# Edge network of a four-layer graph kernel: the head-wise scaling of the message norm in one VectorE operation per tile and head, GpSimd left with the bias

## The reference, cut to what matters

```python
for h in range(4):
    K_v, V_v = x @ Kv2v[h], x @ Vv2v[h]
    K_E, V_E = edge_feature @ Ke2v[h], edge_feature @ Ve2v[h]
    alpha = concatenate([K_v[dst] * K_v[src], K_v[dst] * K_E], axis=1) * scale
    gate = sigmoid(_ln(alpha, ln_g[h], ln_b[h]))
    m = (concatenate([V_v[src], V_E], axis=1) @ Wu[h] + bu[h]) * gate
    m = _leaky(_ln(m @ Wm[h] + bm[h], mln_g[h], mln_b[h]))     # mln_g: norm weight, mln_b: bias
    heads.append(segment_sum(m, dst, num_segments=6250))
out = concatenate(heads, axis=1) @ Wc + bc
```

## Time and profile before

| | |
|---|---|
| time, median of 3 executions | 13212.4 us (13209.07 to 13218.26) |
| time of the profiled execution | 13231.73 us |
| its span, first to last instruction | 13229.9 us |
| busy: TensorE, VectorE, ScalarE, GpSimd | 70%, 67%, 44%, 67% of the span |
| TensorE's mean granted clock | 0.930 |
| edge network, first to last leaky ReLU | 4234.4 to 11287.9 us of the span |

### The profile page before, as it was taken

One profiled execution on the slowest core, in us unless ns is written; L12 is line 12 of the kernel. 1 busy time (PEld: TensorE's weight loads), 2 busy tenths in 40 slices (PEclk: granted clock), 3 DMA queues, 4 the chain that ended last, 5 costly groups with the idle time before them and its releaser, 6 DMA issues.

```text
span 13229.9 us, 180603 instructions
## 1 busy us (share of the span) xinstructions
PE 9252.9 (70%) x45190; PEld 6129.7 (46%) x45190; DVE 8863.8 (67%) x20382; ACT 5824.9 (44%) x11467; POOL 8813.8 (67%) x6219
## 2 busy tenths in 40 slices
PE   1344444444475888888888888888888888669997
PEld 0233333333223665666666665666666656323322
DVE  3233333333206888888888888888888888327896
ACT  0111111111102666666666666666666666006442
POOL 1588888888603888888888888888888888000000
PEclk9999999999997999989999899999999999889997
DMA  9766666666693443434343344344443343569663
GB/s 413 235 157 150 151 152 151 150 152 153 163 416 109 120 119 119 120 119 120 119 120 119 118 120 120 119 120 119 119 120 120 119 119 110 231 279 359 232 219 125
DMA packets 1232544, 2147.28 MB, mean 162 GB/s; under 512 B 345985, under 2 KB 768210, under 8 KB 1218579
## 3 DMA queue, kind: packets, MB, share of 16 engines
q1 hardware_dynamic: 838120, 1657.69, 36.7%
q0 software_dynamic: 390240, 484.27, 16.9%
q10 hardware_dynamic: 4048, 3.51, 0.1%
HBM read 1652.11 MB, written 492.84 MB: 162 GB/s over the span
## 4 chain that ended last, share of the span: by engine, by line
POOL 44%; issue 20%; PE 15%; DMA 8%; DVE 5%; ACT 3%; SPq 3%; POOLq 1%; DVEq 1%; another core or an unknown queue 0%; ACTq 0%; PEldq 0%
POOL arena L1362 22%; POOL adj L1401 14%; POOL arena L1414 6%; PE psum L1273 5%; DMA arena<-adj 4%; DMA adj<-put_val,put_idx 3%; SPq L1453 3%; PE psum L1318 2%; ACT arena L980 2%; POOL arena L1417 1%; PE psum L1131 1%; PE psum L1285 1%; PE psum L1196 1%; PE psum L1209 1%; PE psum L1186 1%
## 5 line engine op out<-in xcount | busy, mean ns | idle before, releaser
L1401 POOL DMA_INDIRECT adj<-put_val,put_idx x1616 | 2638.3, 1633 | 844.9 <-issue 478.1
L980 ACT ACTIVATE arena<-arena 128x128 f32<-128x128 f32 x6464 | 2657.6, 488 | 298.2 <-DVE arena L774 170.4
L1110 PE MATMUL psum<-ke,arena 64*128 64x256 f32 x3232 | 1451.8, 640 | 1883.2 <-DMA arena<-in_edge_t 1883.2
L1362 POOL DMA_INDIRECT arena<-table1q,idx_dst x1616 | 2249.3, 1392 | 492.6 <-issue 492.6
L1362 POOL DMA_INDIRECT arena<-table,idx_blk x1616 | 1903.5, 1178 | 431.5 <-issue 374.9
L1110 PEld LDWEIGHTS psum<-ke,arena 64*128 64x128 f32 x3232 | 1039.7, 329 | 2294.9 <-issue 2025.9
L1196 PEld LDWEIGHTS psum<-wm,arena 128*128 128x128 f32 x12928 | 1755.6, 203 | 608.0 <-issue 509.4
L986 ACT ACTIVATE arena<-psum,cols 128x512 f32<-128x512 f32 x1616 | 1250.0, 774 | 1710.8 <-PE psum L1178 1386.7
L1186 PE MATMUL psum<-arena,wvu 128*128 128x512 f32 x3232 | 1894.1, 671 | 83.0 <-DVE arena L703 60.2
L1209 PE MATMUL psum<-arena 128*128 128x128 f32 x6464 | 1113.3, 325 | 1119.7 <-DVE arena L730 1107.0
L1196 PE MATMUL psum<-wm,arena 128*128 128x64 f32 x12928 | 1798.2, 285 | 5.9 <-issue 4.6
(11 more groups left out here) (208 smaller groups left out, 11727.7 us busy)
## 6 DMA issues: line engine op xcount, KB each, us to landing
arena<-adj SPq DMA_DIRECT2D x192, 1568.0 KB, 12.5
arena<-adj SPq DMA_DIRECT2D x336, 896.0 KB, 4.7
kept_keys<-arena SPq DMA_DIRECT2D x404, 512.0 KB
arena<-kept_keys SPq DMA_DIRECT2D x404, 512.0 KB
adj<-arena SPq DMA_DIRECT2D x98, 1568.0 KB
arena<-in_edge_t SPq DMA_DIRECT2D x808, 128.0 KB
kept_hot<-arena SPq DMA_DIRECT2D x404, 256.0 KB
arena<-kept_hot SPq DMA_DIRECT2D x404, 256.0 KB
```

What stands on the lines that cost most here:

```text
L980: A.activation(to, at_, ACT.Identity, bias=shift[z][:, n:n + 1], scale=rstd[z][:, n:n + 1]).then_inc(normed, 1)
L1110: last = M.matmul(psum[:, 2 + 2 * z + j, t * H * D:(t + 1) * H * D], edge0[z][:, 2 * j + t, :], ke[D:P, :], start=True, stop=True)
L1362: K.indirect_dma_start(out=dst[:, t, :], out_offset=None, in_=table, in_offset=bass.IndirectOffsetOnAxis(ap=idx[:, t:t + 1], axis=0)).then ...
L1401: K.indirect_dma_start(out=adj, out_offset=bass.IndirectOffsetOnAxis(ap=put_idx[s][:, j:j + 1], axis=0), in_=put_val[s][:, j:j + 1], in_of ...
```

## The change

VectorE's one product of 128x1024 (with the inverse deviation, broadcast over each block of 64 columns) becomes 16 operations of 128x64. Each multiplies its block by the inverse deviation as a per-partition scalar and by the 64 norm weights of its head. GpSimd's product with the norm weight goes; its sum with the bias stays. The semaphore counts follow: `chain2` rises by 16 for a group (`C2 = G * H`), `y_affine` by 1.

```diff
-        C2 = 1
+        C2 = G * H
...
-                    dve.wait_ge(y_affine, 2 * (i - 3))
+                    dve.wait_ge(y_affine, i - 3)
...
                 if now[3]:
-                    V.tensor_tensor(y[odd], o_sb[odd], root[:, Q:2 * Q].unsqueeze(2).to_broadcast([P, Q, D]),
-                                    ALU.mult).then_inc(chain2, 1)
+                    for n in range(Q):
+                        h = n % H
+                        V.scalar_tensor_tensor(y[odd][:, n, :], o_sb[odd][:, n, :], root[:, Q + n:Q + n + 1],
+                                               mg[:, h * D:(h + 1) * D], ALU.mult, ALU.mult).then_inc(chain2, 1)
...
                 pool.wait_ge(chain2, C2 * (g + 1))
-                K.tensor_tensor(y4, y4, mg[:, :].unsqueeze(1).to_broadcast([P, G, H * D]),
-                                ALU.mult).then_inc(y_affine, 1)
-                pool.wait_ge(y_affine, 2 * g + 1)
                 K.tensor_tensor(y4, y4, mb[:, :].unsqueeze(1).to_broadcast([P, G, H * D]),
                                 ALU.add).then_inc(y_affine, 1)
```

## The result

The changed kernel takes 13834.7 us (13831.69 to 13839.73), the kernel before 13215.0 us with these runs: 619.7 us more, ratio 1.0471 with a 95% interval of 1.0456 to 1.0485. The forecast was +310 us and slower; the sign and the mechanism on VectorE held, the size did not, and the time lies outside the range (up to 13660).

What follows compares the result with a forecast made beforehand. GpSimd was taken to pace the loop, VectorE 1.09 us a group behind. VectorE's demand, 16.41 - 1.13 + 2.99 = 18.27 us against a period of 17.50, gave +0.77 us times 404, +310 us: 13522 us, range 13240 to 13660.

Steps and rivals of the forecast that it cites:

- GpSimd paces the loop and no more than 1.09 us a group is to be had: Edge network: relieving GpSimd gains at most VectorE's wait for it, 440 us in all; then VectorE sets the pace.
- L784's slot, 1.13 us, goes: VectorE's product with the inverse deviation drops out, saving 1.13 us a group from start to next start.
- Sixteen slots of 0.187 us, 2.99 us: VectorE's new 128x64 operations: each 0.067 us streaming, 0.07 overhead and 0.05 for the column, 2.99 us a group.
- the column: Reading the per-partition scalar from SBUF in each new VectorE operation was taken to add 0.05 us to its slot.
- VectorE's demand: VectorE's own work in the loop: 16.41 us a group before, 18.27 after, with the 139.1 us register-load idle unchanged.
- The waits that move: Edge network: L730's wait for GpSimd goes; GpSimd runs its bias at once, then waits for `chain2` 3 to 5 us a group.
- ScalarE and TensorE count for nothing: Edge network: ScalarE sees `chain2` 1.9 us later but is 66% busy, TensorE only gains time; no cost counted.
- The port counts for nothing: VectorE's sixteen operations fall where GpSimd waits for them, so no cost was counted for the SBUF port shared with GpSimd.
- Rivals 1, 2 and 3: VectorE's slot: column free, -78 us (8%); column's read hidden, +32 us (12%); no overlap between operations, +970 us (4%).
- 4 (gathers among the sixteen): Rival: GpSimd's gathers get among VectorE's sixteen operations, 0.6 us a group more, +555 us, 13765 us; chance 4%.

Runs made afterwards that it cites:

- a_imm: Changed kernel with constant 1.0 in place of the inverse deviation in the sixteen operations; 13428.7 us, 222.0 more than the kernel before.
- b_pad64: Kernel before with 64 one-column VectorE writes put in long before the edge network, its loop unchanged; 13148.0 us, ratio 0.9953.
- two_pad64: Kernel before with deviation and weight as two VectorE products of 128x1024, plus 64 one-column writes ahead; 13364.7 us, ratio 1.0118 to the kernel before.
- split1_pad64: Kernel before with one tile of four's weight product moved to VectorE, plus 64 one-column writes ahead; 13058.8 us, 251.2 more than without the writes.

## Why the prediction was wrong, step by step

- *GpSimd paces the loop and no more than 1.09 us a group is to be had*: right as to this change. L730's wait fell from 440.8 to 0.3 us.
- *L784's slot, 1.13 us, goes*: right.
- *Sixteen slots of 0.187 us, 2.99 us*: measured 0.196 and 3.13. The term that was too small is the column: taken as 0.05, measured 0.060 (`a_imm`). L547's duration, 0.22 us beyond its streaming against 0.16, had it right; I had taken L703's slot instead. This is 0.14 us a group, 57 us. The figure of the Trainium skill ("VectorE: DVE Perf Modes", the TRN2 errata) that would have given 0.127 us is not far from the 0.136 us that `a_imm` shows without a column, but the measured 0.196 decides for this operation.
- *VectorE's demand "includes 139.1 us in all that it idles once in four iterations for its register loads, which the change leaves"*: **this is the step that failed.** The wait was not for the register loads alone: it sits at the branch back of the loop, and the change puts 60 more instructions into each pass and 75 ahead of it, so that the loop came to lie over four blocks of instructions instead of three (worked out from where the packets come). The pause became 391.8 us, 253 more, or 0.63 us a group. `b_pad64` shows that the place alone brings it, `two_pad64` and `split1_pad64` that it then costs 250 us. With it the forecast sum is 310 + 57 + 253 = 620 us.
- *The waits that move*: GpSimd did run the bias at once after the sixteenth operation and idled; 2618.2 / 404 = 6.5 us a group rather than 3 to 5. The rest is its late gathers, most of which have gone. In the page after:

```profile
L1364 POOL DMA_INDIRECT arena<-table1q,idx_dst x1616 | 1620.7, 1003 | 492.7 <-issue 492.7
L1364 POOL DMA_INDIRECT arena<-table,idx_blk x1616 | 1551.6, 960 | 431.9 <-issue 375.5
```

  1003 and 960 ns where there were 1392 and 1178.
- *ScalarE and TensorE count for nothing*: right. TensorE's granted clock fell from 0.930 to 0.887, but VectorE waited less than 4 us for both in the whole edge network.
- *The port counts for nothing*: right for the sixteen operations, which follow each other at 0.196 us; of 6060 such steps none took over 0.221.
- Rivals 1, 2 and 3 (slots of 0.127, 0.144 and 0.29 us) and 4 (gathers among the sixteen) all fell. None of the four had the instruction stream in it.

The kernel before has hardly a packet in its loop, so its trace could not give this price. The Trainium skill ("Runtime: NRT & Kernel Launch", Instruction fetch mechanics) says that a taken branch whose target is outside the window of instructions held makes the engine wait for a DMA fetch. The traces agree as to the mechanism, with a wait of some 2.6 to 2.9 us a branch beyond the 1.4 us that the pause had before. The page has blocks of 16 KiB and a window of two; here the packets have 8.2 KB, the fetches within a pass come some 128 records apart, and loops over three such blocks run free while all over four fetch again. What the exact rule is between the two, the runs leave open, and also whether a loop of 384 could be placed so that it fits.

## What to carry to other kernels

Before adding instructions to a loop, look at the pause at its branch back and at the packets of the instruction queue: here a queue with packets in proportion to the passes meant that the loop was fetched anew each time, and 64 or 68 instructions ahead of it brought that on three times and took it away once, with no change inside. When work is moved to relieve the engine that sets the pace, move only half the distance to the next engine (here one tile of four, 3.0% faster, where all of it in two operations gave 0.7%), and in the fewest operations: sixteen of 64 columns with a scalar column took 3.13 us where the two whole products take 2.27.

## What the runs showed of the hardware that was not expected

- A per-partition scalar read from SBUF cost the scalar_tensor_tensor of 128x64 0.060 us in its slot (0.196 against 0.136), even in a run of sixteen equal ones.
- The place of a loop alone was worth 252 us in 13113 (1.9%), and with GpSimd pacing the loop it had the opposite sign: a longer pause of VectorE made the kernel 59 us faster, since fewer of GpSimd's gathers began under a large two-input operation of VectorE (288 by source where there were 398).
- Late gathers are some 2.7 us of GpSimd's 17.5 us group in the kernel before (four gathers each of 1392 and 1178 ns against 949) and 0.25 us after. In the kernel before every gather that began under L682 (402) or L730 (398) took over 1.1 us, and no other did. So GpSimd's pace was in part VectorE's doing.
